# Last layer of a four-layer graph network: the vector rotations and the scan are placed between the product groups, two products are made one, and both operands of the radial product are padded to 128 rows

## The chip, the cores and the metric

The kernel runs on one core of one Trainium2 chip. The metric is device time in microseconds (us) of one launch; lower is better. Before the change it is 19209.46 us, the median of three runs (19208.34 to 19211.77).

## The reference

There are 12500 nodes with 32 features and 400000 edges sorted by target. Four layers follow each other; each gathers the source node's row for every edge, makes a message, adds the messages of a target, and closes with a residual and a layer norm. Only the last layer changes. Its reference, cut to what matters:

```
R = relu(abs_distances[:, None] @ w1 + b1) @ w2 + b2     # 64 hidden units, 384 radial weights an edge
Y = spherical_harmonics(rel_vec)
Fj = features[src]                                       # 8 scalars and 8 vectors (3 components) an edge
acc = acc + norm_i * einsum('euv,ef,evi,ofi->euo', Rb[..., k], Yf, Fb, C)   # per pair of kinds and order
out = zeros.at[dst].add(msg)
x = layernorm(x + out)
```

The kernel rotates each vector into the edge's own frame. There the tensor product falls apart into 8 x 8 blocks of R, multiplied with the rotated features and summed over v; the sums are rotated back, and a running sum (a scan that is reset where the target changes) adds the messages of a target.

## The kernel before, in words

The 400000 edges lie as 128 partitions x 3125. The last layer walks them in 125 chunks of T = 25 edges a partition (`vector_edges3`, L1017 and on; loops of four chunks, `Fori(0, 31)`). Five engines work on it, each with its own instruction list in a fixed order, joined by semaphores. The order of VectorE is written by hand and numbered: `PER3 = 48` counts a chunk, `v3(c, n)` is the semaphore value of step n of chunk c.

- GpSimd (`gpsimd_chunk3`, L1562) gathers the rows of chunk c with 25 indirect DMAs into one of four buffers `L3.gb`. SyncE (`sync_rows3`, `sync_attr3`, L1718 to L1723) loads the indices, the frames and the distances ahead.
- ScalarE (`scalar_chunk3`) copies the frames into PSUM (`scalar_frames3`, L1248), makes the hidden layer `L3.HS` (`scalar_hidden3`, L1242), lays out `L3.G` (L1255 to L1257), copies scalar sums (L1260), the reset mask (L1263), and the scanned rows (L1268), and starts their store (L1270).
- TensorE (`tensor_chunk3`, L1460) makes R: one fp32 matmul an edge column (25 a chunk), stationary `HS[0:65]` (64 hidden units and a row of ones), moving `w2r` of 65 x 384. Each matmul shows as two instructions in the trace. The 25 columns go in nine groups, eight of 3 and one of 1; groups 0 to 7 alternate between banks 0 to 2 and 3 to 5 of PSUM, group 8 has bank 6. Group g may start when VectorE has finished the products of group g-2.
- VectorE (`vector_chunk3`, then `vector_groups3`) first does the rotations of a chunk: `along` three times (L935, the vectors of chunk c into the frame), the last reduction of the chunk before (L989), two additions (L957, L968), `back` three times (L939, the sums of chunk c-1 out of the frame), an addition (L978), the carry (L979), the addition into the scan's input (L981), and the scan (L985). Then come the nine product groups: for each, a product of 256 columns an edge (L1006), two products of 128 columns (L1010), and, one group late, the reduction over v (L989).

The product groups before, in their order:

```
for g, (t0, n) in enumerate(GROUPS):
    e.wait_ge(sem("pe_r"), c * 25 + (t0 + n + 50))          # TensorE has made group g
    ... L1006: 256 columns x n edges
    for a in range(2):
        ... L1010: 128 columns x n edges
    if g:
        sums(e, g - 1)                                      # L989
```

Of the kernel before, what the change touches and what calls it, by code (L numbers as in the profile page):

```python
# [14 lines left out]
P = 128  # L15
# [67 lines left out]
def gnn_kernel(nc, x, src, dst, ea2, ea3, ea5, ew, ew1, W0, W1, G2, MU, SG, ROOT, BIAS, w1, b1, w2, b2, out):  # L83

    ctx = ExitStack()
    with ctx:
# [56 lines left out]
        w2r = sb("w2r", [65, 384])  # L143
# [211 lines left out]
        L3.sums = cv(T * 32).rearrange("p (t c) -> p t c", t=T)  # L355
        L3.G = cv(T * 48).rearrange("p (t c) -> p t c", t=T)
        L3.gp = [cv(T * 24) for _ in range(3)]
        L3.bp = [cv(T * 24) for _ in range(3)]
# [90 lines left out]
        def vector_ends(e):  # L449
# [47 lines left out]
            wr = w2r[:, :].rearrange("h (b u q v) -> h b u q v", b=3, u=8, q=2)  # L497
# [403 lines left out]
        GR, RED, FIN, SCAN, MUL = 7, 4, (4, 6, 8, 9, 10, 11, 12, 13), 13, 14  # L901
        PER3 = 48

        def v3(c, n):

            return c * PER3 + (mk["base3"] + n)

        def v3_mul(g):

            return 16 if g == 0 else 15 + 4 * g  # L910

        def v3_red(g):
            return 20 + 4 * g

        def vector_chunk3(e, c, i, k):

            begin, ends = not isinstance(i, str), i is not None
            i_ = 0 if i is None else i
            s4, s2, p2 = k % 4, k % 2, (k - 1) % 2
            up = lambda ins: ins.then_inc(dv.up(), 1)  # L920
            prev = lambda n: e.wait_ge(dv.h, v3(c, n))

            def skip(n):
                prev(n - 1)
                e.sem_inc(dv.up(), 1)  # L925

            f_ = L3.gb[s4][:, :, 8:32].rearrange("p t (v j) -> p t v j", v=8)
            gp = [a.rearrange("p (t c v) -> p t c v", t=T, c=3) for a in L3.gp]
            bp = [a.rearrange("p (t u o) -> p t u o", t=T, u=8) for a in L3.bp]
            Gf = L3.G.rearrange("p t (c q v) -> p t c q v", c=3, q=2)[:, :, :, 1]  # L930
            Sv = L3.sums[:, :, 8:32].rearrange("p t (c u) -> p t c u", c=3)
            S = L3.sit[p2][:, :, 8:32].rearrange("p t (u o) -> p t u o", u=8)

            def along(j):
                up(e.tensor_tensor(gp[j], f_[:, :, :, j].unsqueeze(2).to_broadcast([P, T, 3, 8]),  # L935
                                   frp[s2][:, :, :, j:j + 1].to_broadcast([P, T, 3, 8]), ALU.mult))

            def back(q):
                up(e.tensor_tensor(bp[q], Sv[:, :, q].unsqueeze(3).to_broadcast([P, T, 8, 3]),  # L939
                                   frp[p2][:, :, q].unsqueeze(2).to_broadcast([P, T, 8, 3]), ALU.mult))  # L940

            if begin:
                e.wait_ge(sem(f"g3_{s4}"), nth4(i_, k) * 400)
                e.wait_ge(sem("ac_M"), c + 1)
                e.wait_ge(dv.h, v3(c - 1, GR))
                for j in range(3):
                    along(j)
            else:
                for n in range(1, 4):
                    skip(n)  # L950
            if ends:
                last_sums(e, v3(c - 1, v3_mul(8)))
            else:
                skip(4)
            if begin:
                prev(2)
                up(e.tensor_tensor(L3.gp[0], L3.gp[0], L3.gp[1], ALU.add))  # L957
            else:
                skip(5)
            if ends:  # L960
                prev(4)
                e.wait_ge(sem("ac_M"), c + 1)
                back(0)
            else:
                skip(6)
            if begin:
                prev(5)
                up(e.tensor_tensor(Gf, gp[0], gp[2], ALU.add))  # L968
            else:
                skip(7)  # L970
            if not ends:
                for n in range(8, 14):
                    skip(n)
                return
            back(1)
            back(2)
            prev(8)
            up(e.tensor_tensor(L3.bp[0], L3.bp[0], L3.bp[1], ALU.add))  # L978
            up(e.tensor_copy(L3.si[p2][:, :, 0:1], L3.so[s2][:, :, T:T + 1]))  # L979
            prev(10)  # L980
            up(e.tensor_tensor(S, bp[0], bp[2], ALU.add))  # L981
            prev(12)
            e.wait_ge(sem("ac_0"), c)
            e.wait_ge(sem("rowc3"), c)
            up(e.tensor_tensor_scan(L3.sof[p2], L3.mrf[p2], L3.sif[p2], 0.0, ALU.mult, ALU.add))  # L985

        def sums(e, g):
            t0, n = GROUPS[g]
            e.tensor_reduce(L3.sums[:, t0:t0 + n].rearrange("p t c -> p (t c)"),  # L989
                            L3.prod[g % 3][:, 0:n].rearrange("p t (b v) -> p (t b) v", v=16), AX.X, ALU.add).then_inc(dv.up(), 1)  # L990

        def last_sums(e, done):
            e.wait_ge(dv.h, done)
            sums(e, 8)

        def vector_groups3(e, c):
            R = psall[:, :].rearrange("p (b c) -> p b c", c=512)
            for g, (t0, n) in enumerate(GROUPS):
                Rg = R[:, BANK[g]:BANK[g] + n]
                pr = L3.prod[g % 3][:, 0:n]  # L1000
                Gt = L3.G[:, t0:t0 + n]
# [3 lines left out]
                e.wait_ge(dv.h, v3(c, RED) if g == 2 else v3(c, v3_red(g - 3)) if g > 2 else v3(c - 1, v3_red(g + 6)))  # L1005
                e.tensor_tensor(  # L1006
                    pr[:, :, 0:256].rearrange("p t (b v) -> p t b v", v=16), Rg[:, :, 0:256].rearrange("p t (b v) -> p t b v", v=16),
                    Gt[:, :, 0:16].unsqueeze(2).to_broadcast([P, n, 16, 16]), ALU.mult).then_inc(dv.up(), 1)
# [4 lines left out]
                if g:  # L1013
                    e.wait_ge(dv.h, v3(c, v3_mul(g - 1)))
                    sums(e, g - 1)

        def vector_edges3(e):  # L1017
            for a in range(2):
                e.memset(L3.sof[a], 0.0).then_inc(dv.up(), 1)
                e.memset(L3.mr[a][:, :, 0:1], 0.0).then_inc(dv.up(), 1)  # L1020
                e.memset(L3.HS[a][64:65], 1.0).then_inc(dv.up(), 1)
            after(e)
            barrier(e, "vector")
            mk["base3"] = dv.n
            vector_chunk3(e, 0, None, 0)
            vector_groups3(e, 0)
            assert dv.n == v3(1, 0), (dv.n, v3(1, 0))
            with e.Fori(0, 31) as i:
                for k in range(1, 5):
                    vector_chunk3(e, i * 4 + k, i, k)  # L1030
                    vector_groups3(e, i * 4 + k)
            dv.n = v3(125, 0)
            vector_chunk3(e, 125, "end", 125)
            assert dv.n == v3(125, 13)
# [215 lines left out]
        def scalar_chunk3(e, c, i, k):  # L1250
            i_ = 0 if i is None else i
            s4, p2 = k % 4, (k - 1) % 2
            if not isinstance(i, str):
                e.wait_ge(dv.h, v3(c, GR))
                e.activation(L3.G[:, :, 0:8], L3.gb[s4][:, :, 0:8], ACT.Copy)  # L1255
                e.activation(L3.G[:, :, 16:24], L3.G[:, :, 40:48], ACT.Copy, scale=-1.0)
                e.activation(L3.G[:, :, 32:40], L3.G[:, :, 24:32], ACT.Copy).then_inc(sem("ac_G"), 1)  # L1257
            if i is not None:
                e.wait_ge(dv.h, v3(c, RED))
                e.activation(L3.sit[p2][:, :, 0:8], L3.sums[:, :, 0:8], ACT.Copy).then_inc(sem("ac_0"), 1)  # L1260
                e.wait_ge(dv.h, v3(c, SCAN))
            if not isinstance(i, str):
                e.activation(L3.mr[k % 2][:, :, 1:T + 1], mask[:, bass.ds(c * T, T)].unsqueeze(1).to_broadcast([P, 32, T]), ACT.Copy)  # L1263
                scalar_frames3(e, i_, k + 1)
            if i is not None:
                n_ = nth2(0, 124) if isinstance(i, str) else nth2(i, k - 1)
                e.wait_ge(sem(f"rowd3_{p2}"), n_ * 16)
# [3 lines left out]
            if not isinstance(i, str):  # L1271
                scalar_hidden3(e, i_, k + 1, c + 1)
# [585 lines left out]
```

## Time and profile before

| what | value |
|---|---|
| median of three runs | 19209.46 us |
| the profiled execution, device time | 19205.08 us |
| its span | 19203.2 us |
| busy in the span: PE / DVE / ACT / POOL | 35% / 72% / 15% / 67% |
| last layer, first to last scan (L985, 125 of them) | 13792.5 to 18990.2 us |
| VectorE waiting for TensorE at L1006 | 303.6 us in 750 waits |

The span is one execution seen by the hardware profiler. Engines: PE is TensorE's matmuls, PEld its weight loads, DVE is VectorE, ACT is ScalarE, POOL is GpSimd, SP is SyncE. Durations in the timeline reach to an instruction's end; where two follow each other closely, the second starts before the recorded end of the first, so what an instruction costs its engine is the distance from its start to the next start. The granted clock (PEclk) is the share of TensorE's full 2.4 GHz.

### The profile page before, as it was taken

What the parts mean: (1) busy time and instruction counts of PE and PEld (TensorE: products, weight loads), DVE (VectorE), ACT (ScalarE), POOL (GpSimd) and SP (SyncE); (2) the same over time, 40 slices, a digit from 0 to 9 for tenths busy, and PEclk for the clock granted to TensorE, in tenths of its full rate; (3) what the DMA queues carried; (4) which work ended last, traced back from release to release, by engine and by line L of the source; (5) the groups of instructions that cost most, each with busy time, mean ns of one, the idle gap of its engine ahead of it and who ended that gap; (6) DMA issues with size and microseconds to landing.
All of it is one profiled execution on the core that took longest, in us unless ns stands there. A gap on an engine that the chain in (4) does not pass through costs nothing. (4 is left out here: it accounts for less than half of the span.)

```text
span 19203.2 us, 130329 instructions
## 1 busy us (share of the span) xinstructions
PE 6807.9 (35%) x26457; PEld 3964.5 (21%) x26457; DVE 13889.0 (72%) x19625; ACT 2940.0 (15%) x3943; POOL 12799.7 (67%) x13055
## 2 busy tenths in 40 slices
PE   0111111111444544443300000000277777777774
PEld 0000000000333333333200000000143343434342
DVE  4777777773999999987633333333499999999995
ACT  0000000000222222220011111111011111111110
POOL 3777777776777777771177777777666666666654
PEclk9996555555777777775555555555555555555555
DMA  4333333331111111103322222222121112111111
GB/s 109 98 98 96 96 97 96 98 95 22 27 27 28 27 27 28 27 23 123 113 58 59 58 59 59 58 59 59 34 44 41 44 41 44 41 42 43 41 44 24
DMA packets 816139, 1108.01 MB, mean 58 GB/s; under 512 B 441714, under 2 KB 577704, under 8 KB 802673
## 3 DMA queue, kind: packets, MB, share of 16 engines
q0 software_dynamic: 437600, 503.25, 12.1%
q1 hardware_dynamic: 302643, 403.03, 7.6%
q10 hardware_dynamic: 75474, 197.60, 2.8%
q14 instruction: 340, 2.79, 0.1%
q8 instruction: 82, 1.34, 0.0%
HBM read 714.37 MB, written 389.45 MB: 57 GB/s over the span
## 5 line engine op out<-in xcount | busy, mean ns | idle before, releaser
L1584 POOL DMA_INDIRECT s_arena<-d_t,s_arena x6250 | 5903.1, 944 | 2073.5 <-issue 2007.7
L1460 PE MATMUL psall<-s_w2r,s_arena 65*128 65x384 f32 x6250 | 4049.5, 849 | 1439.2 <-DVE s_arena L1010 1208.0
L1562 POOL DMA_INDIRECT s_arena<-d_t,s_arena x3125 | 3189.9, 1021 | 2026.2 <-issue 915.5
L1539 POOL DMA_INDIRECT d_pay<-s_arena x3125 | 3027.0, 969 | 992.3 <-issue 932.6
L1460 PEld LDWEIGHTS psall<-s_w2r,s_arena 65*128 65x128 f32 x6250 | 2092.9, 337 | 3394.7 <-issue 1750.8
L1370 PE MATMUL psall<-s_arena 128*128 128x500 bf16 x1875 | 873.2, 494 | 4188.5 <-DVE s_arena L526 3793.8
L989 DVE TENSOR_REDUCE s_arena<-s_arena 128x96 f32<-128x1536 f32 x1125 | 1826.6, 1624 | 0.4 <-DVEq L925 0.4
L892 DVE TENSOR_TENSOR s_arena<-s_arena,psall 128x2400 f32<-128x2400 f32 x125 | 332.0, 2656 | 1734.7 <-DMA s_arena<-d_t,s_arena 1734.7
L1484 PE MATMUL psall<-s_tails,s_mfix 128*128 128x32 f32 x6 | 1.9, 411 | 3979.4 <-DVE s_tails L1066 3979.4
L1305 ACT ACTIVATE s_arena<-s_arena 128x800 f32<-128x800 f32 x250 | 428.6, 1714 | 6220.3 <-DVE s_arena L1058 6220.3
L1006 DVE TENSOR_TENSOR s_arena<-psall,s_arena 128x768 f32<-128x768 f32 x1125 | 1005.8, 894 | 304.8 <-PE psall L1460 303.6
L1370 PEld LDWEIGHTS psall<-s_arena 128*128 128x128 bf16 x1875 | 199.3, 106 | 4758.9 <-DVE s_arena L526 4207.0
L1387 PE MATMUL psall<-s_ident,s_arena 128*128 128x128 f32 x3125 | 602.8, 321 | 1481.0 <-DVE s_arena L625 1481.0
L1396 PE MATMUL psall<-s_arena 128*128 128x128 f32 x6250 | 1050.5, 317 | 111.1 <-ACT s_arena L1191 104.3
L1010 DVE TENSOR_TENSOR s_arena<-psall,s_arena 128x384 f32<-128x384 f32 x2250 | 1072.3, 519 | 0.0
L827 DVE TENSOR_REDUCE s_arena<-s_arena 128x600 f32<-128x4200 f32 x125 | 1027.1, 8217 | 4.3
L1396 PEld LDWEIGHTS psall<-s_arena 128*128 128x128 f32 x6250 | 904.4, 221 | 306.6 <-DVE s_arena L648 147.7
L526 DVE TENSOR_TENSOR s_arena<-s_arena,psall 128x625 bf16<-128x625 f32 x1250 | 944.8, 800 | 1.0 <-PEq L177 1.0
L1191 ACT ACTIVATE s_arena<-psall 128x512 f32<-128x512 f32 x875 | 482.4, 551 | 2744.5 <-PE psall L1387 2744.5
L817 DVE TENSOR_TENSOR s_arena<-s_arena,psall 128x600 f32<-128x600 f32 x125 | 97.5, 780 | 1085.9 <-DMA s_arena<-d_t,s_arena 1085.9
L1484 PEld LDWEIGHTS psall<-s_tails,s_mfix 128*128 128x128 f32 x6 | 1.5, 310 | 3981.4 <-DVE s_tails L1066 3981.4
L625 DVE TENSOR_TENSOR s_arena<-s_arena,psall 128x1536 f32<-128x1536 f32 x250 | 782.1, 3170 | 4.3
(264 smaller groups left out, 12281.7 us busy)
## 6 DMA issues: line engine op xcount, KB each, us to landing
s_arena<-d_t,s_arena POOLq DMA_INDIRECT x9375, 2.5
d_scan<-s_arena ACTq DMA_DIRECT2D x375, 400.0 KB, 2.6
s_arena<-d_ew SPq DMA_DIRECT2D x126, 800.0 KB, 6.3
s_arena<-d_pay SPq DMA_DIRECT2D x33, 1650.0 KB, 7.3
d_inj<-s_agg SPq DMA_DIRECT2D x125, 400.0 KB, 4.0
s_arena<-d_inj SPq DMA_DIRECT2D x125, 400.0 KB, 3.4
d_pay<-s_arena POOLq DMA_INDIRECT x3125
d_pay<-s_agg SPq DMA_DIRECT2D x100, 429.0 KB, 2.9
```

The costliest lines, as they stand in the source:

```text
L526: return e.tensor_tensor(O[sl], h5[:, :, bass.ds(n, 1)].to_broadcast([P, 5, 125]), iob, ALU.is_equal)
L625: up(e.tensor_tensor(xb[:, t0:t1], so_[:, t0:t1].unsqueeze(2).to_broadcast([P, t1 - t0, 4, 32]), tv[:, t0:t1].unsqueeze(3).to_broadcast([P ...
L827: e.tensor_reduce(S[:, :, 8:32], w7.rearrange("p m t c -> p t c m"), AX.X, ALU.add).then_inc(dv.up(), 1)
L989: e.tensor_reduce(L3.sums[:, t0:t0 + n].rearrange("p t c -> p (t c)"), L3.prod[g % 3][:, 0:n].rearrange("p t (b v) -> p (t b) v", v=16), A ...
L1006: e.tensor_tensor(pr[:, :, 0:256].rearrange("p t (b v) -> p t b v", v=16), Rg[:, :, 0:256].rearrange("p t (b v) -> p t b v", v=16), Gt[:, ...
L1010: e.tensor_tensor(pr[:, :, 256 + 128 * a:384 + 128 * a].rearrange("p t (u v) -> p t u v", u=8), Rg[:, :, 256:384].rearrange("p t (u v) -> ...
L1370: e.matmul(R5s[:, 0:4], lhsT, rhs[:, 0:4], start=start, stop=True, skip_group_check=True)
L1396: m = e.matmul(ps[2 + yb][:, 128 * t:128 * t + 128], S1.xT[yb][:, 128 * t:128 * t + 128], S1.wt, start=True, stop=True)
L1460: e.matmul(ps[BANK[g] + t][:, 0:384], hv_[:, :, t0 + t], w2r[:, :], start=True, stop=True).then_inc(sem("pe_r"), 1)
L1539: e.indirect_dma_start(pay_d, bass.IndirectOffsetOnAxis(ap=S1.adr[s4][:, t:t + 1], axis=0), S1.pay[s4][:, 33 * t:33 * t + 33], None).then_ ...
L1562: e.indirect_dma_start(L3.gb[s][:, t], None, T3_d, bass.IndirectOffsetOnAxis(ap=L3.idx[s][:, t:t + 1], axis=0)).then_inc(sem(f"g3_{s}"), 16)
L1584: e.indirect_dma_start(L.gb[s][:, t * L.CW:(t + 1) * L.CW], None, L.tab, bass.IndirectOffsetOnAxis(ap=L.idx[s][:, t:t + 1], axis=0)).then_ ...
```

## The change

VectorE's order in a chunk is now a list of names, and the values of the semaphore follow from it. `mAg` is the product of 256 columns of group g, `mBg` the other product, `rg` the reduction; `bk`, `ba`, `ca`, `bs`, `sc` are the way back, the carry and the scan of chunk c-1; `al`, `aa`, `ag` are the rotation of chunk c+1, one chunk earlier than before:

```
+        ORDER = ("mA0 mB0 mA1 mB1 r0 bk0 mA2 mB2 r1 bk1 mA3 mB3 r2 bk2 ba mA4 mB4 r3 ca bs mA5 mB5 r4 sc al0 al1 "
+                 "mA6 mB6 r5 al2 aa mA7 mB7 r6 ag mA8 mB8 r7 r8").split()
```

The two products of 128 columns are one instruction, which reads the same 128 columns of PSUM twice:

```
-                for a in range(2):
-                    e.tensor_tensor(
-                        pr[:, :, 256 + 128 * a:384 + 128 * a].rearrange("p t (u v) -> p t u v", u=8), Rg[:, :, 256:384].rearrange("p t (u v) -> p t u v", u=8),
-                        Gt[:, :, 16 + 16 * a:32 + 16 * a].unsqueeze(2).to_broadcast([P, n, 8, 16]), ALU.mult).then_inc(dv.up(), 1)
+                e.tensor_tensor(
+                    pr[:, :, 256:512], Rg[:, :, 256:384].unsqueeze(2).to_broadcast([P, n, 2, 128]),
+                    L3.GE[s2][:, t0:t0 + n].rearrange("p t a v -> p (t a) v").unsqueeze(2).to_broadcast([P, 2 * n, 8, 16]), ALU.mult).then_inc(dv.up(), 1)
```

`L3.sums` and `L3.G` have two buffers each, and `L3.G` is split in `G` (16 columns) and `GE` (32 columns). ScalarE lays them out with five copies in place of three, for chunk c+1, after `ag`:

```
+        def scalar_split3(e, k):
+            G, GE = L3.G[k % 2], L3.GE[k % 2]
+            e.activation(G[:, :, 0:8], L3.gb[k % 4][:, :, 0:8], ACT.Copy)
+            e.activation(G[:, :, 8:16], L3.gv[:, :, 0], ACT.Copy)
+            e.activation(GE[:, :, 0, 0:8], L3.gv[:, :, 2], ACT.Copy, scale=-1.0)
+            e.activation(GE[:, :, 1, 0:8], L3.gv[:, :, 1], ACT.Copy)
+            e.activation(GE[:, :, :, 8:16], L3.gv[:, :, 1:3], ACT.Copy).then_inc(sem("ac_G"), 1)
...
+        def scalar_chunk3(e, c, i, k, first=False, last=False):
+            if not first:
+                scalar_part3(e, c, k)
+            e.activation(L3.mr[k % 2][:, :, 1:T + 1], mask[:, bass.ds(c * T, T)].unsqueeze(1).to_broadcast([P, 32, T]), ACT.Copy)
+            if not last:
+                scalar_hidden3(e, i, k + 1, c + 1)
+                e.wait_ge(dv.h, v3(c, "bk2"))
+                scalar_frames3(e, i, k + 1)
+            if not first:
+                scalar_row3(e, c, i, k)
+            if not last:
+                e.wait_ge(dv.h, v3(c, "ag"))
+                scalar_split3(e, k + 1)
```

The matmul's two operands get 128 rows, of which rows 65 to 127 are zero; the zeros are written once, at the kernel's start and at the layer's start:

```
-        w2r = sb("w2r", [65, 384])
+        w2r = sb("w2r", [P, 384])
+            e.memset(w2r[64:128, :], 0.0).then_inc(dv.up(), 1)
...
+                e.memset(L3.HS[a][64:128], 0.0).then_inc(dv.up(), 1)
+                after(e)
                 e.memset(L3.HS[a][64:65], 1.0).then_inc(dv.up(), 1)
...
-            hv_ = L3.HS[k % 2][0:65].rearrange("h (p t) -> h p t", p=P)
+            hv_ = L3.HS[k % 2].rearrange("h (p t) -> h p t", p=P)
```

The first chunk's rotation stands ahead of the loop (`Fori(0, 30)`), the last four chunks are written out behind it, and the way back of the last chunk follows by itself. GpSimd and SyncE wait for `mA0` of chunk c-4 where they waited for step 14, which was the same product. The temporaries of the way back (`L3.bp`) lie in another SBUF tile, `ta`, of the same kind.

## Rows read from the trace of the kernel before

**Rows 1.** Windows: last layer; layer 1. Busy us (instructions) by engine, granted clock, DMA.
```profile
16000.00:17000.00 1000.00, 770.86 (x1191) 398.62 (x1191) 941.17 (x1146) 173.74 (x192) 609.39 (x595) 0.50 0.19 43
...
5600.00:6400.00 800.00, 391.88 (x2406) 302.65 (x2404) 752.31 (x1049) 189.63 (x334) 608.62 (x629) 0.76 0.12 28
```

**Rows 2.** Instructions and waits of single lines: the scan L985; what L1006 waited for.
```profile
L985 DVE TENSOR_TENSOR_SCAN s_arena<-s_arena x125: 1891/1891/1893, 13792.5 to 18990.2; 128x832 f32<-128x832 f32 x125
...
  PE psall L1460: 303.6, 750
```

**Rows 3.** Timeline of a chunk, rotations and scan: start us, us, engine, line [idle <-releaser].
```profile
14999.97 2.69 DVE L935 TENSOR_TENSOR s_arena<-s_arena,psall 128x600 f32<-128x600 f32 x3
...
15002.58 0.67 DVE L989 TENSOR_REDUCE s_arena<-s_arena 128x32 f32<-128x512 f32 x1
15003.17 0.77 DVE L957 TENSOR_TENSOR s_arena<-s_arena 128x600 f32<-128x600 f32 x1
...
15004.55 0.77 DVE L968 TENSOR_TENSOR s_arena<-s_arena 128x600 f32<-128x600 f32 x1
...
15005.24 1.45 DVE L939 TENSOR_TENSOR s_arena<-s_arena,psall 128x600 f32<-128x600 f32 x2
15005.35 0.37 ACT L1255 ACTIVATE s_arena<-s_arena 128x200 f32<-128x200 f32 x1 [30.00 <-DVE s_arena L968]
...
15006.62 0.77 DVE L978 TENSOR_TENSOR s_arena<-s_arena 128x600 f32<-128x600 f32 x1
15007.32 0.18 DVE L979 COPY s_arena<-s_arena 128x32 f32<-128x32 f32 x1
15007.42 1.31 DVE L981 TENSOR_TENSOR s_arena<-s_arena 128x600 f32<-128x600 f32 x1
...
15008.76 1.89 DVE L985 TENSOR_TENSOR_SCAN s_arena<-s_arena 128x832 f32<-128x832 f32 x1
```

**Rows 4.** Timeline of the same chunk, product groups.
```profile
15010.57 0.93 DVE L1006 TENSOR_TENSOR s_arena<-psall,s_arena 128x768 f32<-128x768 f32 x1
...
15011.42 1.01 DVE L1010 TENSOR_TENSOR s_arena<-psall,s_arena 128x384 f32<-128x384 f32 x2
...
15012.49 32.39 PE L1460 MATMUL psall<-s_w2r,s_arena 65*128 65x384 f32 x50 [9.54 <-DVE s_arena L1010]
...
15016.76 0.96 DVE L1006 TENSOR_TENSOR s_arena<-psall,s_arena 128x768 f32<-128x768 f32 x1 [0.87 <-PE psall L1460]
...
15017.63 1.01 DVE L1010 TENSOR_TENSOR s_arena<-psall,s_arena 128x384 f32<-128x384 f32 x2
...
15018.56 1.74 DVE L989 TENSOR_REDUCE s_arena<-s_arena 128x96 f32<-128x1536 f32 x1
...
15020.68 0.96 DVE L1006 TENSOR_TENSOR s_arena<-psall,s_arena 128x768 f32<-128x768 f32 x1 [0.39 <-PE psall L1460]
...
15039.51 0.41 DVE L1006 TENSOR_TENSOR s_arena<-psall,s_arena 128x256 f32<-128x256 f32 x1
...
15039.84 0.48 DVE L1010 TENSOR_TENSOR s_arena<-psall,s_arena 128x128 f32<-128x128 f32 x2
...
15040.23 1.74 DVE L989 TENSOR_REDUCE s_arena<-s_arena 128x96 f32<-128x1536 f32 x1
...
15041.89 2.70 DVE L935 TENSOR_TENSOR s_arena<-s_arena,psall 128x600 f32<-128x600 f32 x3
```

**Rows 5.** The page's costliest groups: gathers; weight loads of 65 and 128 rows.
```profile
L1562 POOL DMA_INDIRECT s_arena<-d_t,s_arena x3125 | 3189.9, 1021 | 2026.2 <-issue 915.5
...
L1460 PEld LDWEIGHTS psall<-s_w2r,s_arena 65*128 65x128 f32 x6250 | 2092.9, 337 | 3394.7 <-issue 1750.8
...
L1484 PEld LDWEIGHTS psall<-s_tails,s_mfix 128*128 128x128 f32 x6 | 1.5, 310 | 3981.4 <-DVE s_tails L1066 3981.4
```

**Rows 6.** Timeline of the layer's start.
```profile
13706.79 2.73 DVE L1021 MEMSET s_arena<- 1x3200 f32 x1 [0.72 <-issue]
...
13746.64 2.69 DVE L935 TENSOR_TENSOR s_arena<-s_arena,psall 128x600 f32<-128x600 f32 x3 [37.13 <-DMA s_arena<-d_t,s_arena]
```

More of the change, by code:

```diff
@@ L897, in vector_layer2 @@
             e.tensor_reduce(L.sit[s2], L.work.rearrange("p (t q c) -> p t c q", t=T, q=3), AX.X, ALU.add).then_inc(dv.up(), 1)
[L901 to L985, printed above, removed]
@@ new lines, in gnn_kernel, with v3, along3 @@
+        PER3 = len(ORDER)
+        AT3 = {name: n + 1 for n, name in enumerate(ORDER)}
+        BACK3, NEXT3 = ("bk0", "bk1", "bk2", "ba", "ca", "bs", "sc"), ("al0", "al1", "al2", "aa", "ag")
+        def v3(c, name):
+            return c * PER3 + (mk["base3"] + AT3[name])
+        def along3(e, k, j):
+            f_ = L3.gb[k % 4][:, :, 8:32].rearrange("p t (v j) -> p t v j", v=8)
+            return e.tensor_tensor(L3.gp[j].rearrange("p (t c v) -> p t c v", t=T, c=3), f_[:, :, :, j].unsqueeze(2).to_broadcast([P, T, 3, 8]),
+                                   frp[k % 2][:, :, :, j:j + 1].to_broadcast([P, T, 3, 8]), ALU.mult)
@@ new lines, in along @@
+            def along(j):
+                if j == 0:
+                    e.wait_ge(sem(f"g3_{(k + 1) % 4}"), nth4(i, k + 1) * 400)
+                    e.wait_ge(sem("ac_M"), c + 2)
+                    done_before("ag")
+                along3(e, k + 1, j).then_inc(dv.up(), 1)
+            if first:
+                back_ = lambda *names: skip(names)
+            else:
+                back_ = lambda *names: [vector_back3(e, c, k, n) for n in names]
+            mul(0)
+            mul(1)
+            red(0)
@@ new lines, in vector_chunk3 @@
+            back_("bk0")
+            mul(2)
+            red(1)
+            back_("bk1")
+            mul(3)
+            red(2)
+            back_("bk2", "ba")
+            mul(4)
+            red(3)
+            back_("ca", "bs")
+            mul(5)
+            red(4)
+            back_("sc")
+            if last:
+                skip(("al0", "al1"))
+            else:
+                along(0)
+                along(1)
+            mul(6)
+            red(5)
+            if last:
+                skip(("al2", "aa"))
+            else:
+                along(2)
+                done("al1")
+                e.tensor_tensor(L3.gp[0], L3.gp[0], L3.gp[1], ALU.add).then_inc(dv.up(), 1)
@@ new lines, in vector_chunk3, with vector_back3 @@
+            mul(7)
+            red(6)
+            if last:
+                skip(("ag",))
+            else:
+                done("aa")
+                e.wait_ge(sem("ac_G"), c + 1)
+                e.tensor_tensor(L3.gv, L3.gp[0].rearrange("p (t c v) -> p t c v", t=T, c=3),
+                                L3.gp[2].rearrange("p (t c v) -> p t c v", t=T, c=3), ALU.add).then_inc(dv.up(), 1)
+            mul(8)
+            red(7)
+            red(8)
+        def vector_back3(e, c, k, name):
+            s2, p2 = k % 2, (k - 1) % 2
+            if name in ("bk0", "bk1", "bk2"):
+                if name == "bk0":
+                    e.wait_ge(dv.h, v3(c - 1, "r8"))
+                back3(e, k - 1, int(name[2])).then_inc(dv.up(), 1)
+            elif name == "ba":
+                e.wait_ge(dv.h, v3(c, "bk1"))
+                e.tensor_tensor(L3.bp[0], L3.bp[0], L3.bp[1], ALU.add).then_inc(dv.up(), 1)
+            elif name == "ca":
+                e.tensor_copy(L3.si[p2][:, :, 0:1], L3.so[s2][:, :, T:T + 1]).then_inc(dv.up(), 1)
+            elif name == "bs":
+                e.wait_ge(dv.h, v3(c, "ba"))
+                bp = [a.rearrange("p (t u o) -> p t u o", t=T, u=8) for a in L3.bp]
+                e.tensor_tensor(L3.sit[p2][:, :, 8:32].rearrange("p t (u o) -> p t u o", u=8), bp[0], bp[2], ALU.add).then_inc(dv.up(), 1)
+            else:
+                e.wait_ge(dv.h, v3(c, "bs"))
+                e.wait_ge(sem("ac_0"), c)
+                e.wait_ge(sem("rowc3"), c)
+                e.tensor_tensor_scan(L3.sof[p2], L3.mrf[p2], L3.sif[p2], 0.0, ALU.mult, ALU.add).then_inc(dv.up(), 1)
@@ L1023, in vector_edges3 @@
             barrier(e, "vector")
+            e.wait_ge(sem("g3_0"), 400)
+            e.wait_ge(sem("ac_M"), 1)
+            for j in range(3):
+                along3(e, 0, j).then_inc(dv.up(), 1)
+            after(e)
+            e.tensor_tensor(L3.gp[0], L3.gp[0], L3.gp[1], ALU.add).then_inc(dv.up(), 1)
+            after(e)
+            e.tensor_tensor(L3.gv, L3.gp[0].rearrange("p (t c v) -> p t c v", t=T, c=3),
+                            L3.gp[2].rearrange("p (t c v) -> p t c v", t=T, c=3), ALU.add).then_inc(dv.up(), 1)
             mk["base3"] = dv.n
[L1025 to L1028, printed above, removed]
+            vector_chunk3(e, 0, 0, 0, first=True)
+            assert dv.n == mk["base3"] + PER3
+            with e.Fori(0, 30) as i:
                 for k in range(1, 5):
                     vector_chunk3(e, i * 4 + k, i, k)
[L1031 to L1034, printed above, removed]
+            for k in range(1, 5):
+                vector_chunk3(e, 120 + k, 30, k, last=k == 4)
+            dv.n = mk["base3"] + 125 * PER3
+            n = 0
+            for name in BACK3:
+                e.wait_ge(dv.h, mk["base3"] + 125 * PER3 + n)
+                if AT3[name] - 1 > n:
+                    e.sem_inc(dv.h, AT3[name] - 1 - n)
+                vector_back3(e, 125, 125, name)
+                n = AT3[name]
+            dv.n = v3(125, "sc")
         vector_body = {0: vector_layer0, 2: vector_layer2}
@@ L1280, in scalar_edges3 @@
             scalar_hidden3(e, 0, 0, 0)
-            scalar_chunk3(e, 0, None, 0)
-            with e.Fori(0, 31) as i:
+            e.wait_ge(dv.h, mk["base3"])
+            scalar_split3(e, 0)
+            scalar_chunk3(e, 0, 0, 0, first=True)
+            with e.Fori(0, 30) as i:
                 for k in range(1, 5):
                     scalar_chunk3(e, i * 4 + k, i, k)
-            scalar_chunk3(e, 125, "end", 125)
+            for k in range(1, 5):
+                scalar_chunk3(e, 120 + k, 30, k, last=k == 4)
+            scalar_part3(e, 125, 125)
+            scalar_row3(e, 125, 31, 1)
             e.wait_ge(sem("rowd3_0"), 16 * (63 + 1))
@@ L1558, in gpsimd_chunk3 @@
             held(e)
-            e.wait_ge(dv.h, v3(c - 4, MUL))
+            e.wait_ge(dv.h, v3(c - 4, "mA0"))
             held(e)
```

89 lines of the change are left out of this document (45 added, 44 removed).

## The prediction

> **What bounds the kernel now.** I read the busy shares by stage first, then the lines that wait, then one chunk of the last layer in the timeline. In the last layer VectorE is busy 941 of 1000 us, TensorE 771, GpSimd 609, ScalarE 174 [rows 1]. The scans come every (18990.2 - 13792.5) / 124 = 41.92 us, one a chunk [rows 2]. The reader should see that neither engine bounds the whole chunk: they take turns. TensorE streams its 25 matmuls without a gap for 32.39 us and then waits 9.54 us for VectorE's first products [rows 4]; these come late because the rotations and the scan stand ahead of them, from 14999.97 to 15010.57, 10.60 us [rows 3]. After that VectorE is the faster one and waits: 0.87 us before group 2, 0.39 before group 3, then about 0.29 each; over the layer 303.6 us in 750 waits, six a chunk, 2.43 us a chunk [rows 2, 4]. So a chunk is TensorE's 32.4 plus its idle 9.5, and the idle time is VectorE's rotations less what TensorE could make ahead.
>
> **VectorE's work without waits** is the floor once the rotations stand between groups. I take distances from start to start.
> - Rotations, scan and last reduction: 10.60 us [rows 3]. Each instruction stays, with the same shape. The scan waited for the addition right ahead of it (15007.42 to 15008.76, 1.34 us, where the addition lasts 1.31); now products and a reduction stand between them. Other neighbours start 0.08 before the recorded end, so about 0.1 goes: 10.50.
> - A full group: the large product 0.87 (15016.76 to 15017.63), the two small ones 0.93 together (15017.63 to 15018.56), the reduction 1.66 (15040.23 to 15041.89) [rows 4].
> - The merged product has 768 elements, as the large one has; both read PSUM and an operand repeated in the middle. I give it 0.87, so 0.06 goes a group. From below it can hardly be cheaper than the large product (0.85 after the scan, 15010.57 to 15011.42); from above the nearest patterns that walk unfavourably are `along`, 2.61 us for 1800 elements (1.45 ns each, so 1.11 us for 768), and the strided addition L981, 1.34 for 600 (1.72 us for 768) [rows 3, 4]. The middle dimension repeats whole runs of 128, which resembles neither, so I stay at 0.87 and keep the ends for rivals.
> - The one-column group: 0.33 for its large product (15039.51 to 15039.84), 0.39 for the two small ones, which become 0.33 [rows 4].
>
> Sum: 10.50 + 8 x (0.87 + 0.87 + 1.66) + 0.66 = 38.36 us; with the product at 0.865 it is 38.3. That is 3.6 below 41.92.
>
> **TensorE between these.** Group 2 may start when the small products of group 0 end. Before, that was 15011.42 + 1.01 = 15012.43, and the first product of group 2 came at 15016.76, so 4.33 us pass for three matmuls and the hand-over [rows 4]. In the new order VectorE fills this stretch with mA1 0.87, mB1 0.87, r0 1.66 and bk0 0.69: 4.09, less the recorded tail of 0.07. So 0.3 us of wait stays at group 2, if TensorE keeps its clock. Every later group has a second reduction and a rotation in the same stretch, at least 5.06 us, and TensorE works at 3.84 a group (25 matmuls in 32.39), so no other wait. Its total of 32.4 is under 38.3. I laid the two orders side by side through a chunk with these distances: 38.6 with the half clock, 38.3 with the full one.
>
> **The padding.** The granted clock is 0.50 throughout the last layer, that is 1.2 GHz, though TensorE streamed 32 us without a gap; in layer 1, with operands of 128 rows and TensorE busy 49%, it was 0.76, between its two levels [rows 1]. The pair allows that 128 rows lift the clock; it doesn't prove it. Zero rows make no instruction longer as far as rows show: a weight load of 128 x 128 took 310 ns, one of 65 x 128 took 337 [rows 5]. So the padding is worth between nothing and the 0.3 us, 0 to 37 us in all. I take the middle. By the Trainium skill (TensorE: Matmul & The Clock Gate, Part 1) sustained matmul activity releases the throttle, and rows have no part in it; by that the layer should have run at the full level already, which [rows 1] contradict at 0.50. Read strictly, it leaves the padding at nothing and the sum at the half-clock end.
>
> **What else moves.** ScalarE now makes five copies after `ag` in place of three: at most some 2 us (one lasts 0.37 [rows 3]), beside mA8, mB8, r7 and r8, 2.9 us of VectorE. ScalarE waited 30.00 us there before [rows 3], and its mask, hidden layer, frames and scanned row are done by about 27 us of the chunk, long before `ag` at 35, so nothing on its queue holds the copies. If it were late, each us late would cost a us a chunk. GpSimd's gathers take (3189.9 + 915.5) / 125 = 32.8 us a chunk [rows 5], under 38.3; VectorE needs a chunk's rows some 14 us earlier than before, and a gather ran more than a chunk ahead. Their start waits for an index load that SyncE issues behind the frames and distances; these now depend on `bk2` and on the hidden layer, both earlier in a chunk than the old copies. Only chunk 1 is short: its rows land about 33 us after those of chunk 0 and VectorE would want them after 19 and a rotation, so it waits some 8 us once. On the other side the first chunk has no way back and the last no rotation; with the tail written out, all chunks outside the 123 steady ones come to 81 us against 83 before, the 8 included. At the layer's start two more memsets of 3200 elements stand on the path, 2.73 each and a short wait [rows 6]; with the small one at the kernel's start and two more copies ahead of the first product I add 8 us.
>
> **The sum.** Half clock: 123 x (41.92 - 38.6) = 408, plus 2, less 8: 402 us saved. Full clock: 123 x (41.92 - 38.27) = 449, so 443. From the profiled execution's 19205.1 us that gives 18803 and 18762; the median of the runs is 4.4 above it, so 18807 and 18766. I predict 18785.
>
> **Rivals.**
> - *The merged product saves nothing or a little less, or small waits remain* (0.93 in place of 0.87, or TensorE late at two or three groups): 0.5 to 1.5 us a chunk given back. 18850 to 18970. For it: a new pattern with a repeat in a PSUM read, which no row shows. Against: each small product already repeated its other operand at full rate. 11%.
> - *Slower: the merged product runs at the rate of the strided addition.* Place: nine times a chunk between two products on the engine that now bounds. At 1.72 us a group it adds 0.85 x 8.3 = 7.1 us: 45.4 a chunk, 3.4 over 41.92, so about 19630. It turns the sign from 1.30 us for a full group on ((41.92 - 38.3) / 8.3 + 0.87). At `along`'s rate (1.11) it would still be faster, 38.3 + 2.0, about 19020. For it: three of the shapes in [rows 3] run well over one ns an element. Against: these have strides of several elements inside; here every inner run is 16 or 128 long, as in the large product. 5% for the slower side, 3% for the middle.
> - *The change doesn't do what it says*: TensorE stays the clock of the chunk because group g still waits for group g-2. For it: six waits a chunk before. Against: with a rotation in the stretch VectorE needs 4.78 or more where TensorE needs 3.84. It would leave 41.9, no change. 2%.
> - *Removed instructions are worth their full length.* By the Trainium skill (VectorE: DVE Perf Modes, the TRN2 errata section) an fp32 two-operand instruction takes (N + 151) / 0.96 ns, and one less saves 157 ns. As a mechanism of this kernel: if the second product started only when the first had ended, two of 0.55 would be 1.10. The trace has the pair ending after 1.01 and costing 0.93 to the next start [rows 4]; it agrees with the lengths and not with the spacing. With 157 for the 61 I used, 0.1 x 9 x 123 = 107 us more go: 18680. 3%.
>
> **How the numbers follow.** My case, VectorE without a break but for group 2, has 76% and its own range of 18740 to 18840: a tenth of a us a chunk on either side of the two clock ends, and the uncertain start. The range of 8 in 10 takes in the small-give-back rival's near part: 18725 to 18880. A measurement of this kernel tells about 0.2%, 38 us, from no change. Faster: 76 + 11 + 3 + 3 = 93%. Same: 2%. Slower: 5%.
>
> **What would show it.** Scans every 38.3 to 38.7 us. VectorE busy 99% of the layer, and of the 303.6 us of waits for TensorE at most 40 left, at group 2, or none if the clock is over 0.5 there. The merged product with 768 elements at about 958 ns, 0.87 to the next start. TensorE's gap of 9.5 us replaced by short ones for the small products. GpSimd's 32.8 us of gathers unchanged. Wrong if the merged product is longer, if VectorE waits for ScalarE's copies at mA0 or for gathers at al0, or if the periods stay above 39.

## The result, and the profile after

The changed kernel takes 18780.74 us (median, 18776.28 to 18782.46, four runs) against 19208.9 us of the kernel before (the median of four runs, the three named at the start and one more): ratio 0.9778, 95% interval 0.9761 to 0.9795, 428 us less. The forecast was 18785 us. The profiled execution took 18780.07 us, its span is 18778.3 us.

The page after, for the whole span; 40 slices, tenths of busy time, and the granted clock:

```profile
PE 5929.7 (32%) x26457; PEld 3816.1 (20%) x26457; DVE 13743.4 (73%) x18503; ACT 3023.8 (16%) x4191; POOL 12860.4 (68%) x13055
...
DVE  4777777772999999997933333333379999999995
...
PEclk9999965555777777776555555555567777777776
```

The same windows as in [rows 1], in the last layer of the kernel after:

```profile
16000.00:17000.00 1000.00, 661.07 (x1307) 406.41 (x1306) 996.84 (x1018) 206.38 (x260) 678.91 (x653) 0.78 0.21 46
...
14000.00:18400.00 4400.00, 2911.29 (x5740) 1786.92 (x5739) 4385.57 (x4473) 908.71 (x1143) 2992.93 (x2876) 0.78 0.21 46
```

VectorE is busy 99.7% of the time (94% in [rows 1]), and the granted clock went from 0.50 to 0.78. The scans and the large product's waits, as in [rows 2]:

```profile
L1034 DVE TENSOR_TENSOR_SCAN s_arena<-s_arena x125: 1868/1883/1903, 13828.5 to 18565.2; 128x832 f32<-128x832 f32 x125
...
L946 DVE TENSOR_TENSOR s_arena<-psall,s_arena x1125: 404/952/994, 13766.3 to 18556.6; 128x768 f32<-128x768 f32 x188
its engine sat idle before it (us, times) until:
  PE psall L1518: 16.6, 64
  ACT s_arena L1295: 1.7, 1
```

The last scan stands behind the last chunk's products by itself, only 18.1 us after the one before it, so it is left out of the period: 124 scans start from 13828.5 to 18547.1 us, and a chunk takes (18547.1 - 13828.5) / 123 = 38.36 us. In the kernel before the period without the last interval (39.0 us) is 41.94. Of the 303.6 us of waits for TensorE 16.6 are left, in 64 waits: 60 of them, 15.0 us, stand before the product of group 2, about one in every second chunk, and the other four in the first chunk. One chunk in the timeline (some lines of it; the columns are those of [rows 3]):

```profile
15992.42 0.96 DVE L946 TENSOR_TENSOR s_arena<-psall,s_arena 128x768 f32<-128x768 f32 x1
...
15993.29 0.96 DVE L949 TENSOR_TENSOR s_arena<-psall,s_arena 128x768 f32<-128x768 f32 x1
...
15994.15 0.96 DVE L946 TENSOR_TENSOR s_arena<-psall,s_arena 128x768 f32<-128x768 f32 x1
...
15995.88 1.75 DVE L958 TENSOR_REDUCE s_arena<-s_arena 128x96 f32<-128x1536 f32 x1
...
15997.54 0.78 DVE L925 TENSOR_TENSOR s_ta<-s_arena,psall 128x600 f32<-128x600 f32 x1
...
15998.33 0.96 DVE L946 TENSOR_TENSOR s_arena<-psall,s_arena 128x768 f32<-128x768 f32 x1
...
16013.55 1.74 DVE L958 TENSOR_REDUCE s_arena<-s_arena 128x96 f32<-128x1536 f32 x1
...
16015.21 1.88 DVE L1034 TENSOR_TENSOR_SCAN s_arena<-s_arena 128x832 f32<-128x832 f32 x1
...
16017.01 1.83 DVE L919 TENSOR_TENSOR s_arena<-s_arena,psall 128x600 f32<-128x600 f32 x2
...
16020.62 3.32 PE L1518 MATMUL psall<-s_w2r,s_arena 128*128 128x384 f32 x6 [2.44 <-DVE s_arena L949]
...
16028.98 0.53 ACT L1295 ACTIVATE s_arena<-s_arena 128x400 f32<-128x400 f32 x1
...
16030.69 0.96 DVE L946 TENSOR_TENSOR s_arena<-psall,s_arena 128x768 f32<-128x768 f32 x1
```

From 15992.42 to 16030.69 VectorE has no gap: 38.27 us. A chunk with the wait at group 2 has 0.25 us more, which gives the mean of 38.36. The merged product L949 follows after 0.87 and gives way after 0.86 (15994.15 - 15993.29). TensorE's single gap of 9.54 us [rows 4] is now a short one before each burst. ScalarE's last copy ends at 16029.51, 1.18 us ahead of the product that waits for it.

### The profile page after: what moved, and what is told of

Same layout as the page of the kernel before. It is cut to its first block and busy times, and to the rows that moved or that the text cites. A ratio compares the mean times of both kernels' runs of the same rounds, so it can differ in the third digit from the quotient of the medians.

```text
span 18778.3 us, 129812 instructions
## 1 busy us (share of the span) xinstructions
PE 5929.7 (32%) x26457; PEld 3816.1 (20%) x26457; DVE 13743.4 (73%) x18503; ACT 3023.8 (16%) x4191; POOL 12860.4 (68%) x13055
## 5 line engine op out<-in xcount | busy, mean ns | idle before, releaser
L1620 POOL DMA_INDIRECT s_arena<-d_t,s_arena x3125 | 3250.5, 1040 | 1547.9 <-issue 915.1
L1518 PE MATMUL psall<-s_w2r,s_arena 128*128 128x384 f32 x6250 | 3175.2, 667 | 1873.9 <-DVE s_arena L949 1636.5
L1518 PEld LDWEIGHTS psall<-s_w2r,s_arena 128*128 128x128 f32 x6250 | 1946.9, 324 | 3101.8 <-DVE s_arena L949 2225.9
L946 DVE TENSOR_TENSOR s_arena<-psall,s_arena 128x768 f32<-128x768 f32 x1125 | 1007.0, 895 | 19.6 <-PE psall L1518 16.6
L949 DVE TENSOR_TENSOR s_arena<-psall,s_arena 128x768 f32<-128x768 f32 x1125 | 1002.2, 891 | 0.0
```

What stands on the lines that cost most here:

```text
L946: e.tensor_tensor(pr[:, :, 0:256].rearrange("p t (b v) -> p t b v", v=16), Rg[:, :, 0:256].rearrange("p t (b v) -> p t b v", v=16), L3.G[s ...
L949: e.tensor_tensor(pr[:, :, 256:512], Rg[:, :, 256:384].unsqueeze(2).to_broadcast([P, n, 2, 128]), L3.GE[s2][:, t0:t0 + n].rearrange("p t a ...
L1518: e.matmul(ps[BANK[g] + t][:, 0:384], hv_[:, :, t0 + t], w2r[:, :], start=True, stop=True).then_inc(sem("pe_r"), 1)
L1620: e.indirect_dma_start(L3.gb[s][:, t], None, T3_d, bass.IndirectOffsetOnAxis(ap=L3.idx[s][:, t:t + 1], axis=0)).then_inc(sem(f"g3_{s}"), 16)
```

## Experiments

**How the twelve runs are compared.** They came in three sets, on chips 8 (e1, e2, e3, e8), 15 (e4, e5, e6, e9) and 12 (f0, f1, f2, f4). In these sets the kernel before took 22357, 22302 and 22296 us, not 19209: there every layer is longer, the three unchanged ones too. Which chip the first runs had is not on record, so it is not shown whether the chip or something else makes this difference; below, "the first runs" are the two kernels at 19209 and 18781 us, and "the later runs" these twelve. The numbers in microseconds that were expected were worked out for the first runs. So two things are read from each run: the ratio to the kernel before of the same set, and the last layer's profile. The same kernel in two sets differed by 0.0015 (e1 and f1), 0.0002 (e2 and f2) and 0.0020 (e4 and f4) in its ratio, so small differences count only within a set. From the profile come the period (distance of the scans in a window) and VectorE's work a chunk, which is its busy share in that window times the period. An instruction that a wait follows keeps its recorded tail of 0.08 us in the busy share, so the work is too large by that much for each wait in a chunk: the kernel before, with six waits, shows 39.48 us where e2 and f2, with the same instructions on VectorE and fewer waits, show 39.07. With this in mind the work belongs to the kernel and not to the set: 38.2 to 38.3 us for the changed kernel in both.

| run | ratio to before (95%) | period, us | VectorE's work, us | clock |
|---|---|---|---|---|
| before, first runs | | 41.94 | 39.48 | 0.50 |
| changed, first runs | 0.9778 (0.9761 to 0.9795) | 38.36 | 38.23 | 0.78 |
| f0 changed | 0.9938 (0.9921 to 0.9954) | 41.67 | 38.32 | 0.76 |
| f1 changed, 65 rows | 0.9955 (0.9938 to 0.9971) | 41.69 | 38.37 | 0.50 |
| e1 the same, chip 8 | 0.9970 (0.9958 to 0.9981) | 42.14 | 38.34 | 0.50 |
| e2 before, 128 rows | 0.9886 (0.9869 to 0.9902) | 40.57 | 39.07 | 0.80 |
| f2 the same, with f0 | 0.9884 (0.9867 to 0.9900) | 40.43 | 39.06 | 0.80 |
| e3 changed, two products | 0.9990 (0.9980 to 0.9999) | 42.49 | 38.92 | 0.74 |
| e8 before, one product | 0.9991 (0.9982 to 1.0001) | 42.51 | 38.64 | 0.50 |
| e5 lumps, 128 rows | 0.9893 (0.9876 to 0.9909) | 40.50 | 38.57 | 0.80 |
| e6 lumps, 65 rows | 1.0090 (1.0063 to 1.0117) | 45.56 | 38.75 | 0.50 |
| e4 changed, copy on ScalarE | 0.9926 (0.9910 to 0.9943) | 41.32 | 37.84 | 0.77 |
| f4 the same, with f0 | 0.9906 (0.9889 to 0.9922) | 41.04 | 37.86 | 0.76 |
| e9 e4 and vectors on ScalarE | 0.9965 (0.9953 to 0.9978) | 41.89 | 37.30 | 0.78 |

The window rows behind the last two columns, 17000 to 21500 us, of f0, f1, f2, f4 in this order; busy us of PE, PEld, DVE, ACT, POOL, then the clock:

```profile
17000.00:21500.00 4500.00, 2793.73 (x5399) 1682.47 (x5399) 4137.91 (x4211) 856.28 (x1079) 2762.07 (x2702) 0.76 0.19 42
```

```profile
17000.00:21500.00 4500.00, 3662.06 (x5400) 1758.56 (x5400) 4142.10 (x4210) 857.83 (x1080) 2781.20 (x2700) 0.50 0.19 42
```

```profile
17000.00:21500.00 4500.00, 2364.15 (x5576) 1710.50 (x5574) 4347.13 (x5343) 805.18 (x889) 2817.63 (x2781) 0.80 0.20 44
```

```profile
17000.00:21500.00 4500.00, 2818.56 (x5486) 1708.98 (x5484) 4151.09 (x4275) 1018.13 (x1202) 2784.10 (x2738) 0.76 0.20 43
```

**The changed kernel itself.**

> The changed kernel itself, beside the three below. The eight runs so far came with a kernel before at 22300 to 22360 us, where every layer took longer than in the first profile, and the changed kernel was not among them; this gives them their reference. If that chip is met again, the changed kernel should stand at about 22000 (by VectorE's work alone; the other waits of a chunk, some 2 to 3 us, come on top of any order); if the first one is, at 18780.

22162.11 us, 133 below the kernel before of its set: a third of the gain of the first runs, and 160 us slower than expected for such a chip. VectorE's work is the same to 0.1 us; the rest of the period is waiting, which in the first runs was 0.1 us and here is 3.3. Where, in the profile of f0 (the first fence is what L946 waited for, the second a piece of the timeline):

```profile
its engine sat idle before it (us, times) until:
  remote: 401.7, 91
  PE psall L1518: 36.0, 64
  issue: 33.6, 20
```

```profile
19002.00 0.70 SPq L1780 DMA_DIRECT2D s_arena<-d_y  x1
19003.41 0.01 SPq L1781 DMA_DIRECT2D s_arena<-d_ew  x1
19003.55 0.96 DVE L946 TENSOR_TENSOR s_arena<-psall,s_arena 128x768 f32<-128x768 f32 x1 [3.64 <-remote]
...
19005.43 4.21 PE L1518 MATMUL psall<-s_w2r,s_arena 128*128 128x384 f32 x6 [6.17 <-DVE s_arena L949]
```

The wait stands before mA4, the product after `bk2` and `ba`, and so do 73 of the 79 waits of this kind in the window from 17000 to 21500 us (307.9 of 321.9 us). Its matmuls are not what is late here, for TensorE had been idle for 6.17 us by 19005.43. "remote" means that the profile shows no releaser. SyncE's own instructions are irregular in f0 too: its register moves at the distances' load took 2 to 792 ns against 29 to 38 in the first runs (min/median/max, f0 first, the changed kernel of the first runs second):

```profile
L1781 SPq MOVE s_arena<-d_ew x124: 2/12/792, 16693.7 to 21881.5; - x124
```

```profile
L1781 SPq MOVE s_arena<-d_ew x124: 29/29/38, 13736.8 to 18463.1; - x124
```

What holds VectorE there stays open; the runs don't tell whether it is a sequencer, the load or the chip. In f1 the waits at the same product are as long (306.1 us in 90 waits), and 57 of them are put down to TensorE.

**The padding in the new order.**

```
-            hv_ = L3.HS[k % 2].rearrange("h (p t) -> h p t", p=P)
+            hv_ = L3.HS[k % 2][0:65].rearrange("h (p t) -> h p t", p=P)
-                    e.matmul(ps[BANK[g] + t][:, 0:384], hv_[:, :, t0 + t], w2r[:, :], start=True, stop=True).then_inc(sem("pe_r"), 1)
+                    e.matmul(ps[BANK[g] + t][:, 0:384], hv_[:, :, t0 + t], w2r[0:65, :], start=True, stop=True).then_inc(sem("pe_r"), 1)
```

> The changed kernel with the matmul's operands cut back to 65 rows (the zeros are still written). My theory: VectorE without waits bounds the chunk, and TensorE's clock only decides a small wait at group 2. The clock then shows 0.50 in the last layer again, a chunk takes 38.5 to 38.6 us instead of 38.2, and the time is 18815 us (+35). Rival A, the padding carries the gain: the periods go back above 40 us and the time is over 19000. Rival B, rows have nothing to do with the clock: it stays at 0.78 and the time at 18781.

> The changed kernel with 65 rows in the matmul, beside the changed kernel. My theory: clock back to 0.50, 0.3 us a chunk more, +35 us where the chunk is otherwise undisturbed. If other waits delay TensorE, the half clock has less to hide them with and the padding is worth more: up to 1 us a chunk, +125. Rival (rows have nothing to do with the clock) is already out: the clock was 0.50 in the run before.

The clock was 0.50 in both, and TensorE's bursts took 1.3 us a matmul again (12 in 15.75 us in one of f1). In f1 VectorE waits 0.25 us at group 2 in every chunk (108 waits, 27.1 us, in the window), in f0 in every second one (51 waits, 12.8 us): that is the predicted wait, and it is worth 0.13 us a chunk or 16 us between the two clocks. The time of f1 was 22191.64 us, 29.5 more than f0, where 35 were expected; the intervals of the two ratios overlap, and the periods of the two profiles differ by only 0.02 us, so the size is not firm. The sign set for "the padding carries the gain", a period above 40 us, can't be read here, because the changed kernel itself is above it; what f0 and f1 show is that the padding is at most a small part of the 133 us in this order. "Rows have nothing to do with the clock" is out. In the first runs this kernel was not tried with 65 rows.

**The padding in the old order.**

```
-        w2r = sb("w2r", [65, 384])
+        w2r = sb("w2r", [P, 384])
-            hv_ = L3.HS[k % 2][0:65].rearrange("h (p t) -> h p t", p=P)
+            hv_ = L3.HS[k % 2].rearrange("h (p t) -> h p t", p=P)
```

> The kernel before with nothing but the padding to 128 rows. If 128 rows lift the clock, TensorE makes a group of three in 2 to 3 us where VectorE needs 3.46, the waits before groups 2 to 7 (2.43 us a chunk) go, and a chunk takes VectorE's 39.1 to 39.4 us without waits: about 18870 us, so that the padding alone would bring four fifths of the change's gain. If the gap of 9.5 us a chunk keeps the clock low, or rows don't matter, only the memsets are added: 19215 us.

> The kernel before with the padding alone, beside both kernels. Where the chunk is undisturbed, VectorE's waits for TensorE go and a chunk takes 39.1 to 39.4 us: 18870 us against 19209, four fifths of the whole gain. If the clock falls during TensorE's gap and the first groups are late, 39.5 to 40 us: 18930 to 18970.

The clock rose to 0.80, although TensorE still has a long gap in each chunk (14.10 us in one of f2), and the waits of the later groups went:

```profile
19020.42 8.40 PE L1464 MATMUL psall<-s_w2r,s_arena 128*128 128x384 f32 x18 [14.10 <-DVE s_arena L1008]
```

The time was 22038.86 us, 257 below the kernel before and 123 below the changed kernel of the same set; the intervals don't touch. In the profile of f2 the chunk is VectorE's 39.06 us and 1.4 of waits, 0.75 at group 2 and 0.58 at group 3, the first ones after the gap. A chunk of 39.1 to 39.4 was expected, or 39.5 to 40 with the first groups late; 40.4 was found, with the first groups late. What these chips' waits put on it can't be taken out, so under the conditions of the first runs this kernel lies, by an estimate from 39.06 us of work and up to 1.4 of waits, 180 to 350 us below the kernel before. It was not run there, so how much of the 428 us the padding alone would have brought is not shown.

**The merged product, taken out of the new order and put alone into the old one.**

```
-                e.tensor_tensor(
-                    pr[:, :, 256:512], Rg[:, :, 256:384].unsqueeze(2).to_broadcast([P, n, 2, 128]),
-                    L3.GE[s2][:, t0:t0 + n].rearrange("p t a v -> p (t a) v").unsqueeze(2).to_broadcast([P, 2 * n, 8, 16]), ALU.mult).then_inc(dv.up(), 1)
+                for a in range(2):
+                    e.tensor_tensor(
+                        pr[:, :, 256 + 128 * a:384 + 128 * a].rearrange("p t (u v) -> p t u v", u=8), Rg[:, :, 256:384].rearrange("p t (u v) -> p t u v", u=8),
+                        L3.GE[s2][:, t0:t0 + n, a].unsqueeze(2).to_broadcast([P, n, 8, 16]), ALU.mult).then_inc(dv.up(), 1)
```

> The changed kernel with the merged product split into its two halves again, order and padding kept. My theory: VectorE is the bound and each split costs the difference in spacing, 0.06 us a group, so 9 x 0.06 = 0.55 us a chunk: +68 us, 18849. Rival (what a removed instruction is worth is its fixed part in full, 157 ns): +174 us, 18955. Rival (TensorE or ScalarE bounds after all): no difference.

VectorE's work rose from 38.32 us (f0) to 38.92 us, 0.60 a chunk, where 0.55 was expected and a removed instruction at its full fixed part would give 9 x 0.157 = 1.4. The time went from 0.9938 to 0.9990 of the kernel before, about 116 us in two different sets, of which 0.60 x 124 = 74 is work; the rest is waits, and what two sets differ by.

> The kernel before with nothing but the two products made one (65 rows, old order; ScalarE makes five copies as in the changed kernel, on its old place). TensorE clocks groups 2 to 7 there, so what the merging saves in them turns into waiting; only the groups ahead of TensorE's restart save: 0.1 to 0.15 us a chunk, while the two more copies stand ahead of the first product, behind the scan, and cost nothing. 19190 us, at most 20 below the kernel before. Rival: it saves the full 0.5 us a chunk, 19140.

The same edit in the old order, with ScalarE's five copies: ratio 0.9991, some 20 us, not told apart from nothing, as expected. The work fell by 0.8 to 38.64 us, of which about 0.3 is the tails of the waits that are gone (3.4 a chunk against six), so that 0.5 to 0.6 is the merging. That the saving turned into waits for TensorE is argued and not shown: the window of e8 has 361.8 us of them in 267 waits, but no profile of the kernel before was taken in the later runs.

**The place of the rotations.** The order of e5 and e6; the calls in the body follow it:

```
ORDER = "mA0 mB0 mA1 mB1 r0 bk0 bk1 bk2 ba ca bs sc mA2 mB2 r1 mA3 mB3 r2 mA4 mB4 r3 mA5 mB5 r4 mA6 mB6 r5 "
        "mA7 mB7 r6 mA8 mB8 r7 r8 al0 al1 al2 aa ag"
```

> The changed kernel with the rotations back in two lumps: the whole way back and the scan between r0 and mA2, and the rotation of the next chunk after r8; 128 rows and merged product kept. VectorE's work is the same. If its work bounds at the raised clock, the place doesn't matter: 38.3 to 38.5 us a chunk (two neighbours depend on each other again, 0.1 to 0.2 us), 18785 to 18805. If the spreading matters, it is over 18850. ScalarE's copies are now exposed between ag and the next mA0, about 1.7 us a chunk: if they can't hide, +210 us, 18990.

> The same two lumps with 65 rows. TensorE at 1.2 GHz needs 3.84 us a group and VectorE 3.40 between two of them, so TensorE falls behind in groups 3 to 7: by my distances 39.0 us a chunk with hidden copies, and as much more as the copies are exposed (1.7 us, which at the same time let TensorE catch up). The difference to the run with 128 rows shows what the clock is worth in this order: 0.4 to 0.7 us a chunk if mine is right, 50 to 90 us in all, against 35 in the spread order. Rival: no difference, since the copies hide TensorE's lag.

With 128 rows: period 40.50 us, work 38.57, and nearly all that is between stands before mA0 in these two rows of the waits of e5 (17000 to 21500 us); all 111 chunks have one:

```profile
DVE s_arena L946 <- ACT s_arena L1285: 133.8, 72, 1.9
DVE s_arena L946 <- issue: 72.5, 39, 1.9
```

That is 1.86 us each time: ScalarE's five copies, exposed, as expected (1.7). So what the spreading buys at the raised clock is not TensorE's time but the cover for these copies: 1.9 us a chunk. In the later runs it cost more than it bought: the lumps with 128 rows took 22067.14 us, 79 below e4, the better form of the spread order in the same set (the intervals don't touch). The spread order has the unexplained waits, about 3 us a chunk in e4 as in f0; the lumps with 128 rows have none of them. In the first runs the lumps were not tried.

With 65 rows the kernel took 22536 us, 469 more than with 128 in the same set, 3.8 us a chunk, and is slower than the one before. (Its four runs lie between 22446 and 22644 us, and the profile, with a period of 45.56 us, is of the slowest.) That is far over the 0.4 to 0.7 expected. At groups 6 and 7, where TensorE falls behind, the waits are 61.9 us in the window, 0.6 a chunk, as expected; but 417.8 us in 86 waits, 4.2 a chunk, stand before mA1, 28 of them (183.6 us) without a releaser, and how much of these is the clock stays open. The direction is clear: in lumps the clock matters (469 us), spread it hardly does (29.5).

**A version with less work on VectorE.**

```
-                e.tensor_tensor(L3.sit[p2][:, :, 8:32].rearrange("p t (u o) -> p t u o", u=8), bp[0], bp[2], ALU.add).then_inc(dv.up(), 1)
+                e.tensor_tensor(L3.bp[0], L3.bp[0], L3.bp[2], ALU.add).then_inc(dv.up(), 1)
+            e.activation(L3.sit[p2][:, :, 8:32], L3.bp[0].rearrange("p (t f) -> p t f", t=T), ACT.Copy).then_inc(sem("ac_T"), 1)
```

> The changed kernel; the addition that writes the scan's input with a stride (1.24 us) writes a dense tile (0.69), and ScalarE copies it into the scan's layout. If VectorE's work is the bound, 0.55 us a chunk goes: 18713 us. If another engine holds the chunk now, nothing: 18781. If ScalarE's copy comes late for the scan (it has mA5, mB5 and r4, 3.4 us), it is slower.

> The changed kernel with the strided addition of the scan's input made dense on VectorE and laid out by ScalarE, beside the changed kernel. VectorE's work is the bound, so 0.55 us a chunk goes: 68 us below the changed kernel where the chunk is undisturbed (18713). If the scan now waits for ScalarE's copy (one more hand-over between engines), it is no faster or slower.

22091.10 us, 71 below the changed kernel of the same set (68 expected; the intervals touch at 0.992). The work fell by 0.46 us (f4) to 0.48 (e4), not 0.55. This is the best form of the spread order here; the padded old order stayed 52 us below it, with overlapping intervals.

```
+            e.activation(L3.fv[k % 2], L3.gb[k % 4][:, :, 8:32].rearrange("p t (v j) -> p t v j", v=8), ACT.Copy).then_inc(sem("ac_F"), 1)
-            f_ = L3.gb[k % 4][:, :, 8:32].rearrange("p t (v j) -> p t v j", v=8)
+            f_ = L3.fv[k % 2]
```

> The run before it, and ScalarE also copies the gathered vectors component by component into a dense tile ahead of the three along products, which now take 0.87 us each where the back products of the same size take 0.69. If the stride of 12 bytes in the gathered rows makes them slow, they fall to 0.69 and 0.54 us a chunk goes: 18647 us. If the repeated frame element in PSUM makes them slow, they stay and the time is that of the run before, 18713.

The work fell by another 0.54 us to 37.30, and a product's recorded length from 955 to 767 ns: the 12-byte stride of the gathered rows, not the repeated element in PSUM, made these products slow. The time did not follow: 22224.78 us against 22145.95 of e4, since VectorE's waits without a releaser rose from 329.7 to 476.4 us in the same window. The first saving still showed in the time (71 us in f4), this one did not.

## Why the prediction was right, point by point

- *VectorE's work as the floor.* 38.27 to 38.36 us were worked out from spacings of the kernel before; the chunk shows 38.27 without a gap and the windows give 38.23. On that rests the result, and e3 and f4 moved the work by about what the spacings said (0.60 for 0.55, 0.46 for 0.55). The scans come every 38.36 us, inside the 38.3 to 38.7 named as the sign.
- *The merged product.* Given 0.87 us; it is 0.87 and 0.86 to the next start. The stride rival (1.11 or 1.72) did not occur. Nor did the full fixed part: e3 measured 0.60 / 9 = 67 ns a merge for the 61 used. By an estimate from the formula of the Trainium skill (VectorE: DVE Perf Modes, the TRN2 errata section) it would be 157 ns; the formula's length for 768 elements, 957 ns, is near the 958 recorded before the change, but the spacings don't follow it.
- *TensorE between.* A wait of 0.3 us at group 2 at half clock, none at the full one; 60 of 125 chunks have one of 0.25, which is what a clock between the levels would give, and f1 at 0.50 has it in every chunk. The rival on TensorE reads one number wrong: with one `back` in the stretch VectorE needs 1.66 + 0.69 + 0.87 + 0.87 = 4.09 us and not 4.78; it still exceeds TensorE's 3.84, so nothing hangs on it.
- *The clock.* I took the middle of its two ends without being able to say that it rises. It rose from 0.50 to 0.78 with 128 rows, and was 0.50 again with 65 in e1 and f1. That the rows would do this was not known, only allowed for. In the new order it is worth 16 us by the waits and 29.5 by the times, both inside my 0 to 37.
- *ScalarE's copies.* At most 2 us under 2.9; they ended 1.18 us early. e5 shows the price without cover, 1.86 us a chunk.
- *Gathers.* (3250.5 + 915.1) / 125 = 33.3 us a chunk by the page after, against the 32.8 of [rows 5]; hidden. The first chunk's wait was 4.85 us, not 8.
- *Outside the steady chunks.* I added 8 us and took off 2. From the layer's first memset to its first product it took 57.0 us (13709.26 to 13766.25) against 51.6 before: 5.4 more.

The closeness of 18781 to 18785 is in part luck: the steady chunks gained 123 x (41.94 - 38.36) = 440 us where the middle of the forecast's two ends has 428, and the layers before the last, in which the change does nothing but one memset at the start, ran 8.5 us longer in this profile. What the prediction did not see is that the gain depends on the conditions of the run: in the later runs a third of it was left, for a reason that stays open. And it named the padding as worth at most 37 us, which holds in the new order alone; in the old one it was worth 257 us in the later runs. The two parts buy largely the same thing: the raised clock takes away the waits that the spreading hides. In the later runs the spreading and the merging, put on top of the padding, made the kernel 123 us slower. So the mechanism is shown, VectorE without waits at the sum of its own spacings; that the reordering was needed for it is not shown, because no part was run by itself under the conditions of the first runs.

## What to carry to other kernels

When two engines take turns at being late in a fixed order, add up the later bound's own spacings, start to start, from an undisturbed stretch: that sum is the new period where nothing else waits (38.27 for 38.36 here), and as the engine's work it held to 0.1 us in the later runs too. Before work is reordered to hide a slow engine, try what makes that engine faster by itself; here two tiles padded with zeros did it, and in the later runs that small edit beat the whole reordering. A gain that consists of removed waits has to be measured on more than one chip.

## What the runs showed of the hardware

- A stream of fp32 matmuls with operands of 65 rows stayed at the granted clock 0.50 (1.2 GHz) although it ran 32 us without a gap; the same stream with 63 rows of zeros added got 0.74 to 0.80, with one gap of 14 us in a chunk (f2) as with several short ones (f0). It holds in all 14 profiles of the last layer: five with 65 rows, nine with 128.
- The same program took 19209 us in the first runs and 22296 to 22357 us, 16% more, on chips 8, 12 and 15, with VectorE's spacings unchanged (0.87 and 0.86 us for the two products in f0) and waits for which the profile has no releaser (401.7 us at one line in f0). The cause is not shown.
- A 600-element product whose input has a stride of 12 bytes costs 0.87 us to the next start; three of them on a dense copy take 0.54 us less together (e4 to e9).
